# Moving the last denominators to GpSimd, one cast ahead of an exponential, and five small VectorE instructions into a later wait

## What is computed

```python
scores = jnp.einsum('bhmk,bhnk->bhmn', Q, K)              # 16 heads x 64 tokens, 6272 keys
attn = jax.nn.softmax(scores / np.sqrt(D_K), axis=-1)     # needs the sum of the exponentials of a row
ctx = jnp.einsum('bhmn,bhnv->bhmv', attn, V)
...
temp = jax.nn.softplus(logit_temp) + 1e-06                # "temperature"
probs = jax.nn.softmax(logits / temp, -1)
o = o + jax.nn.sigmoid(conv_res_logit)[None, None, :, None] * local_short   # "residual gate"
```

## Time and profile before

| | |
|---|---|
| median of 3 runs | 410.98 us (410.65 to 411.49) |
| profiled execution, own time | 409.92 us |
| its span | 408.0 us, mean granted TensorE clock 0.992 |
| busy shares | PE 94%, DVE 72%, ACT 71%, POOL 55% |
| first attention | about 21 to 173 us of the span |
| second attention | about 211 to 353 us of the span |

### The profile page before, as it was taken

One profiled execution on the slowest core, in us unless ns is written; L12 is line 12 of the kernel. 1 busy time (PEld: TensorE's weight loads), 2 busy tenths in 40 slices (PEclk: granted clock), 3 DMA queues, 4 the chain that ended last, 5 costly groups with the idle time before them and its releaser, 6 DMA issues.

```text
span 408.0 us, 11595 instructions
## 1 busy us (share of the span) xinstructions
PE 383.0 (94%) x4632; PEld 297.0 (73%) x4632; DVE 292.7 (72%) x762; ACT 287.8 (71%) x568; POOL 223.9 (55%) x163
## 2 busy tenths in 40 slices
PE   6988999999998999988989999999999999999995
PEld 3446777777777778867966777777777779878874
DVE  2788888888876777666767767987887777553544
ACT  3477888888787887646429998889988987444240
POOL 2497989999974655001006897877887661030000
PEclk9899999999999999998999999999999999999999
DMA  8899998989999998990004999999999999700000
GB/s 306 322 253 158 209 178 140 180 144 208 230 173 227 231 173 139 345 396 7 3 2 76 185 207 211 188 193 192 195 187 193 188 203 178 289 2 3 3 2 3
DMA packets 188390, 68.56 MB, mean 168 GB/s; under 512 B 183200, under 2 KB 183984, under 8 KB 187440
## 3 DMA queue, kind: packets, MB, share of 16 engines
q1 hardware_dynamic: 188048, 66.77, 81.6%
q10 hardware_dynamic: 288, 1.05, 0.7%
HBM read 21.90 MB, written 0.03 MB: 54 GB/s over the span
## 4 chain that ended last, share of the span: by engine, by line
PE 45%; DVE 23%; ACT 8%; DMA 8%; issue 7%; POOL 7%; SPq 1%; POOLq 0%; DVEq 0%; ACTq 0%
PE ps L521 16%; PE ps L489 13%; DVE probs L628 10%; DMA probsT<-halves 6%; POOL halves L591 4%; ACT probs L558 3%; DVE probsT L657 3%; PE ps L501 2%; PE ps L1096 2%; DMA moe<-in_ctxT 2%; ACT halves L565 2%; DVE U L646 2%; PE ps L763 1%; DVE halves L591 1%; PE ps L1203 1%
## 5 line engine op out<-in xcount | busy, mean ns | idle before, releaser
L591 POOL TENSOR_TENSOR halves<-probs,halves 128x896 f16<-128x896 f32 x75 | 141.7, 1893 | 60.8 <-ACT halves L565 59.5
L521 PE MATMUL ps<-ctxN,probsT 128*128 128x128 f16 x2352 | 149.0, 219 | 3.1 <-DMA probsT<-halves 2.5
L521 PEld LDWEIGHTS ps<-ctxN,probsT 128*128 128x128 f16 x2352 | 139.5, 98 | 16.7 <-issue 4.8
L489 PE MATMUL ps<-ctxT_parts,GT_parts 128*128 128x512 f16 (+1 forms) x660 | 143.0, 353 | 7.0 <-DVE negmax L628 6.8
L558 ACT ACTIVATE probs<-probs,shifted 128x896 f32<-128x896 f32 x112 | 115.7, 1033 | 7.3 <-DVE shifted L633 7.3
L489 PEld LDWEIGHTS ps<-ctxT_parts,GT_parts 128*128 128x128 f16 x660 | 59.4, 98 | 56.6 <-DVE negmax L628 9.3
L565 ACT CAST halves<-probs 128x896 f16<-128x896 f32 x93 | 86.0, 925 | 0.0
L646 DVE SCALAR_TENSOR_TENSOR U<-U,alpha,ps 128x128 f32<-128x128 f32 x112 | 38.6, 345 | 49.9 <-PE ps L521 49.5
L628 DVE CUSTOM_DVE_ANT_0 probs<-ps,zero,negmax 128x896 f32<-128x896 f32 x56 | 67.5, 1205 | 2.0 <-POOL halves L591 1.6
L628 DVE CUSTOM_DVE_ANT_0 probs<-ps,maskb,negmax 128x896 f32<-128x896 f32 x56 | 67.5, 1205 | 1.6 <-issue 0.7
L555 ACT ACTIVATE alpha<-negmax 128x1 f32<-128x1 f32 x96 | 28.4, 296 | 37.5 <-DVE negmax L628 36.1
(11 more groups left out here) (367 smaller groups left out, 383.4 us busy)
## 6 DMA issues: line engine op xcount, KB each, us to landing
moe<-in_ctxT SPq DMA_DIRECT2D x7, 448.0 KB, 7.6
moe<-in_mask SPq DMA_DIRECT2D x6, 448.0 KB, 10.2
moe<-in_gateT SPq DMA_DIRECT2D x2, 1024.0 KB, 9.2
moe<-in_upT SPq DMA_DIRECT2D x2, 1024.0 KB, 10.9
moe<-in_downT SPq DMA_DIRECT2D x2, 1024.0 KB, 12.4
moe<-in_fir_long SPq DMA_DIRECT2D x1, 2048.0 KB, 10.1
probsT<-halves SPq DMA_TRANSPOSE x93, 4.7
wv<-in_wv SPq DMA_DIRECT2D x2, 512.0 KB, 6.8
```

Source lines behind the costliest of these rows:

```text
L489: ins = pe.matmul(ps[:, 2 * b + h, 0:width], GT_parts[:, g_part, r * P:(r + 1) * P], ctxT_parts[:, keys:keys + width], start=(g_part == 0 ...
L521: ins = pe.matmul(ps[:, bank, 0:D], probsT_parts[:, b, p_part, k * P:(k + 1) * P], ctxN_parts[:, at:at + D], start=(p_part == 0 and c_part ...
L591: eng.tensor_tensor(halves_of(L, n)[:, 1, :], probs[:, n % BUFS, :], halves_of(L, n)[:, 0, :], ALU.subtract).then_inc(lower_of(L, n)[0], 1)
```

## The change

1. The denominators and inverses of the last chunk move from DVE to POOL in both attentions (`last_denominator`): per row tile one TENSOR_SCALAR and one TENSOR_TENSOR with the exponent -1.0 (`ALU.pow`), in place of DVE's TENSOR_SCALAR and RECIPROCAL. `pows` gets a third column for it.
2. In the second attention ACT casts the upper half of tile 1 before the exponential of tile 2, not after it.
3. `residual_gate` and `temperature` leave steps 20 and 22 of the second attention and stand behind the layer norm ahead of the convolutions.

```diff
         def flash_act(act, L):
...
                 if i == 0:
                     g_upper_act(act, L)
                     upper(0)
-                if 2 <= i <= STEPS and not on_pe(L, i - 1):
+                if L and i == 1:
+                    upper(1)
+                if L + 2 <= i <= STEPS and not on_pe(L, i - 1):
                     upper(i - 1)
...
+        def last_denominator(pool, L, n):
+            r = slice(n % RT, n % RT + 1)
+            pool.wait_ge(sem("exp_done"), L * STEPS + n + 1)
+            pool.wait_ge(sem("den_added"), L * STEPS + n)
+            pool.tensor_scalar(den[:, r], den[:, r], alpha[:, n:n + 1], chunksum[:, n:n + 1], ALU.mult,
+                               ALU.add).then_inc(sem("den_added"), 1)
+            pool.wait_ge(sem("den_added"), L * STEPS + n + 1)
+            pool.tensor_tensor(rden[:, r], den[:, r], pows[:, 2:3], ALU.pow).then_inc(sem("den_inverted"), 1)
...
             def add(n):
-                r, c = n % RT, n // RT
-                if c == CH - 1:
-                    dve.wait_ge(sem("exp_done"), base + n + 1)
-                    dve.wait_ge(sem("den_added"), base + n - RT + 1)
-                    dve.tensor_scalar(den[:, r:r + 1], den[:, r:r + 1], alpha[:, n:n + 1], chunksum[:, n:n + 1],
-                                      ALU.mult, ALU.add).then_inc(sem("den_added"), 1)
+                r = n % RT
                 dve.wait_ge(sem("pv_done"), base + n + 1)
...
-                    if i - ADD_LAG >= (CH - 1) * RT:
-                        invert((i - ADD_LAG) % RT)
...
                 denominators(pool, 0, n)
+                if n > (CH - 1) * RT:
+                    last_denominator(pool, 0, n - 1)
...
+            last_denominator(pool, 0, STEPS - 1)
...
                         denominators(pool, 1, n)
+                        if n > (CH - 1) * RT:
+                            last_denominator(pool, 1, n - 1)
...
+                    last_denominator(pool, 1, STEPS - 1)
...
-            flash_dve(dve, 1, {1: partial(g_lower_dve, dve, 1, slice(4 * P, 8 * P), 5), 20: residual_gate,
-                               22: temperature})
+            flash_dve(dve, 1, {1: partial(g_lower_dve, dve, 1, slice(4 * P, 8 * P), 5)})
...
             norm_dve(dve, seq, 4)
+            residual_gate()
+            temperature()
             dve.wait_ge(sem("d_act"), D_ACT["qk"])
```

More of the change, by code:

```diff
@@ L310, in build @@
         orn = sb("orn", [P, 2])
-        pows = sb("pows", [P, 2])
+        pows = sb("pows", [P, 3])
         wamx = sb("wamx", [P, 2 * FT])
@@ L648, in add @@
                     sem("u_added"), 1)
-            def invert(r):
-                dve.wait_ge(sem("den_added"), base + (CH - 1) * RT + r + 1)
-                dve.reciprocal(rden[:, r:r + 1], den[:, r:r + 1]).then_inc(sem("den_inverted"), 1)
             def turned_lower(n):
@@ L1361, in _ @@
             pool.memset(U[:], 0.0).then_inc(sem("cleared"), 1)
-            pool.memset(pows[:], -0.5)
+            pool.memset(pows[:, 0:2], -0.5)
+            pool.memset(pows[:, 2:3], -1.0)
             pool.memset(negmax[:, 0:RT], 3e38).then_inc(sem("cleared"), 1)
@@ L1463, in _ @@
             pool.wait_ge(sem("d_msq"), 1)
-            pool.tensor_tensor(orn[:], oms[:], pows[:], ALU.pow).then_inc(sem("d_mrn"), 1)
+            pool.tensor_tensor(orn[:], oms[:], pows[:, 0:2], ALU.pow).then_inc(sem("d_mrn"), 1)
             norm_pool(pool, 5)
```

## The result

| | before | changed |
|---|---|---|
| median, same chip | 411.03 us (11 runs, 409.6 to 412.25) | 409.18 us (11 runs, 408.37 to 409.85) |
| ratio to before | | 0.9949, 95% interval 0.9933 to 0.9965 |
| profiled execution, own time | 409.92 us | 409.08 us |
| its span | 408.0 us | 407.3 us |

The change makes the kernel faster by 0.51%, 0.35 to 0.67% (2.1 us, 1.4 to 2.8; the medians of the table, taken by themselves, lie 1.85 us apart). The forecast was 409.2 us, with 1.75 us gained. The two profiled executions differ by 0.8 us only: that of before was 1.1 us quicker than its median, that of the changed kernel 0.1. So totals are compared here by timed ratios, and single steps by the traces.

The account below looks back on a forecast made before the run. PE, busy 94% of the span, was taken as the bound, so only its waits pay. 0.35 + 0.70 + 0.70 = 1.75 us off 410.98 gave 409.2 us; forecast band 408.6 to 409.8 (0.63), 8-in-10 range 408.2 to 410.7.

Parts of the forecast that it names:

- Part 2, 0.35: Start of the second attention: the earlier cast brings the whole pace forward by 0.25 to 0.46 us, 0.35 taken.
- Part 3, 0.70: Steps 20 to 23, second attention: moving five small DVE instructions gains 0.80 us, less 0.1 for a late transpose.
- The first aside: The gate's DVE instructions at step 20, second attention: hidden behind another wait, so removing them is worth 0.
- the 0.94 us behind POOL's end: Second attention: DVE's lower half of tile 19 ends 0.94 us after POOL's of tile 18, whenever it starts.
- nothing in POOL's queue depends on the aside: Steps 20 to 22: given as why DVE's lower half ends at 262.42 whenever it starts; first aside worth 0.
- the second aside: The temperature's DVE instructions at step 22, second attention: nothing hides them, so removing them gains 0.80 us.
- Part 1, 0.70: Ends of both attentions: denominator pairs of 0.90 us on POOL end PE's wait for DVE, 0.35 us gained each.
- the term is steep: Ends of both attentions: three pairs stand ahead of tile 52, so 1.2 us a pair loses 0.5 per attention.
- POOL becomes the bound: Rival, chance 0.06: at both ends a pair takes 1.7 us, product 54 comes 2.0 late, time about 413.9.
- The gain is eaten: Rival, chance 0.19: pairs of about 1.2 us lose 0.5 at both ends, or transposes take back; about 410.7 us.
- All comes back: Rival, chance 0.12: both asides count in full (1.41), start gives 0.46, ends 0.96; 2.8 us gained, 408.2.
- Transposes take the pace back: Second attention, alternative within the 0.19 rival: late transposes cost 0.3 at tile 21, or leave part 2's lower end.

Follow-up runs that it names:

- e11: The changed kernel itself measured and profiled once more, nothing edited: 410.2 us, ratio to before 0.9958.
- e2: The kernel before with only the cast of tile 1 put ahead of the exponential of tile 2: 410.0 us, ratio 0.9977.
- e1: The kernel before with only the last chunk's denominators and inverses moved to POOL: 409.5 us, ratio 0.9973.
- e3: The kernel before with only residual_gate and temperature moved behind the layer norm: 410.41 us, ratio 0.9989.
- e9: The changed kernel with only residual_gate back at step 20 of the second attention: 409.69 us, ratio to before 0.9942.
- e8: The changed kernel with only temperature back at step 22 of the second attention: 409.42 us, ratio to before 0.9938.
- e10: The changed kernel with each attention's eight denominator pairs replaced by three 128x8 operations behind the last exponential: 409.56 us, ratio to before 0.9949.
- e4: The changed kernel with one more unused power ahead of each denominator pair on POOL: 409.8 us, ratio to before 0.9974.
- e5: The changed kernel with two more unused powers ahead of each denominator pair on POOL: 412.61 us, ratio to before 1.0032.
- e6: The changed kernel with POOL's denominators of chunks 0 to 4 two steps later: 409.93 us, ratio to before 0.9963.

## Why the prediction was right, and which step of it was not

**The sum.** 1.75 us were forecast, 2.1 (1.4 to 2.8) and, in e11, 1.7 (0.9 to 2.6) measured. The three terms were 0.35, 0.70 and 0.70. Each is found about as large at its own place. That the total is right as well is shown only as a total: only part 1 is seen to reach the end of the kernel, and how much of the measured gain is each part's stays open. Some of the agreement may be luck.

**Part 2, 0.35.** Its chain of causes holds row by row. Product 0 came 0.44 earlier, in the upper part of 0.25 to 0.46, and product 2 by 0.57 (e2) to 0.70. Up to product 9 transposes took 0.13 to 0.65 of it back. But e1 and e3, without the cast, lost 0.35 and 0.58 there too, so most of that isn't the cast's. Up to product 9 the eleven profiles with the cast stand at -0.30 in the mean, the three without (before, e1, e3) at +0.21: a net 0.5, somewhat more than was booked (from single profiles that differ by up to 0.55 among themselves). What the prediction had looked for at tile 2 came at tile 4: in all eleven its transpose was issued 1.9 to 2.2 us behind that of tile 3, not 2.6, and took 6.1 to 6.5 us instead of 4.4.

**Part 3, 0.70.** 0.79 and 0.80 at the marks where the transpose of tile 18 was short, as the working had it before its 0.1 for a late transpose; 0.29 in e11, where it was long (tile 18 and not tile 21). The nine profiles with both asides gone have -0.58 there in the mean, the three with both in place +0.08: 0.66, near the 0.70 booked. What is left of it at product 48 is not shown (see e3). The working treats a step won in the middle of an attention as won for the kernel; it leaves 0 to 0.3 us for one late transpose, and the profiles have several. The first aside is worth 0, as the prediction chose (e9), and the 0.94 us behind POOL's end held in all fourteen profiles. A sub-step failed, that "nothing in POOL's queue depends on the aside": true for the lower half of tile 18, false for that of tile 20. So the 0.80 isn't the second aside's alone; by itself it is worth 0.40 (e8). The two were removed together, so the sum stood. The new place cost 0.0 (DVE was idle 1.45 us behind it, 1.1 had been said).

**Part 1, 0.70.** 0.66 at the marks, 0.81 in e1, 0.29 in e11. The pair took 0.97 us where 0.90 was taken, the TENSOR_SCALAR alone 0.34 and not 0.20. DVE's addition is gone from the chain and PE's own 1.17 us a tile has its place: products 52 and 54 stand 2.34 us apart at both ends in all eleven profiles with part 1, where the kernel before has 2.92 and 2.82 (e2 2.87 and 2.82, e3 2.89 and 2.61). That is -0.58 and -0.48 (e10's expectation has 0.39 for the second), and 0.1 to 0.45 us of it is lost ahead of products 50 and 52 (changed kernel, e1, e11).

The step that failed is "the term is steep": a pair of 1.2 us was to cost 0.5 per attention, and one of 1.7 us 2.0. It took the transpose of tile 52 as 5.4 us whenever it is issued. e4 and e5 showed it at 4.4 and 4.0 when issued later, so that a pair of 1.5 us costs 0.25 to 0.42 and one of 2.0 us 1.3 to 1.6. The rival "POOL becomes the bound" was priced at 413.9 for 1.7 us, with 1.25 us as the point of no gain and 1.4 as slower; at 2.0 us the time is 412.6, and the point of no gain is about 1.7.

**The rivals.** "The gain is eaten" did not come, since the pair stayed at 0.97. "All comes back" would have been 2.8 us, the top of the interval; its share of 0.61 for the first aside is refuted by the stall of 0.47 us that is left, and by e9. "Transposes take the pace back", in the first rival, did happen in part: 0.13 to 0.65 us up to product 9, and late ones further on.

## What to carry to other kernels

Small work that an idle engine takes over is paid for by the engine's next big instruction, not by its busy share: count how many such pieces stand ahead of the one that somebody waits for. Lengthened by 0.5 and 1.1 us they cost 1.3 and 3.5 us here (e4, e5). Putting them behind it or into one batch gained a few tenths of a us at the marks here, and nothing that the times could tell. When two stalls stand in a row, test them apart before one is called free, because the first can set when the second one's blocker starts. And where the next link is a transfer, don't add its usual latency to a new start: issued half a us closer to the one ahead, the transpose of tile 18 took 2 us longer; issued 3.3 us later, that of tile 52 took 1.5 us less. A wait removed in the middle of a pipeline is a gain at that place; follow it to the end of the stage before it is booked for the kernel.

## What the runs showed of the hardware

- DVE's lower half of tile 19 (128x896, two SBUF inputs), begun while POOL's 128x896 one was running, ended 0.94 to 0.95 us after it in all fourteen profiles, whether it lasted 1.23, 1.46 or 1.85 us. The kernel's other DVE lower halves that met none lasted 1.08 us at the shortest. The first instructions of the asides ended with POOL's; DVE's shift of line 633 (128x1, one input) was not held: it took 0.15 us at 258.04 in the kernel before, while POOL's lower half ran from 257.23 to 259.12. POOL is blocked in turn: the product of two 128x8 tiles that takes 0.20 us took 1.05 beside DVE's lower half (e6).
- The same transpose of 128x1792 f16 landed 3.9 to 6.8 us after its issue. For tile 18 it was 4.1 to 4.3 us when issued 2.1 to 2.4 us behind that of tile 17 (five profiles) and 5.8 to 6.4 when issued 1.6 to 2.0 behind (nine). For tile 4 it was 4.4 to 4.5 at 2.5 us and more, 6.1 to 6.5 at 2.2 and less. For tile 46 of the first attention the distance was 1.4 us in short and long ones alike, so the distance isn't the whole rule; what is wasn't found.
- POOL's power took longer with each element: 0.55 us for 128x1, 0.70 for 128x2 (line 1473 of the changed kernel) and 1.67 for 128x8 (e10), where its products of 128x8 took 0.20. One batch of eight (2.4 us with its two forerunners) is still under a third of eight pairs (7.8).
